# Attention scores from two fp32r parts of q and k instead of three bf16 parts, with the two kinds of scores in opposite halves of TensorE's rows

## The reference, cut to what matters

```python
qkv = jnp.einsum('bysd,ed->byse', x, w_qkv) + b_qkv          # (8, 1, 512, 768), fp32
q, k, v = jnp.split(qkv.reshape(B, S, 16, 48).transpose(0, 2, 1, 3), 3, axis=-1)
logits = jnp.einsum('bhqd,bhkd->bhqk', q, k) / math.sqrt(16)
vals = jnp.einsum('bhqk,bhkd->bhqd', jax.nn.softmax(logits, axis=-1), v)
out = jnp.einsum('bse,oe->bso', vals, w_out) + b_out
```

## Time and profile before

| | |
|---|---|
| median of three runs | 1222.1 us |
| the profiled execution | 1222.89 us, its span 1221.0 us |
| stage 1, projections | 0 to about 108 us |
| attention, 32 units | 108 to about 502 us; units 0 to 29 from 108.06 to 474.06 us |
| recurrence and shared expert | about 502 to 836 us |
| routed experts | 836 to 1221 us |
| PE busy, whole span | 1157.2 us (95%) |
| DVE, ACT, POOL busy | 800.3, 505.6, 395.0 us |
| granted TensorE clock, mean | 0.985 |

### The profile page before, as it was taken

How to read it: one execution, slowest core, us unless ns; L and a number is a source line. 1 busy time by engine, 2 the same in 40 slices (tenths; PEclk the granted TensorE clock), 3 DMA queues, 4 the chain that set the end, 5 groups by cost and what they waited for, 6 DMA issues and landing times.

```text
span 1221.0 us, 20443 instructions
## 1 busy us (share of the span) xinstructions
PE 1157.2 (95%) x5606; PEld 696.1 (57%) x5607; DVE 800.3 (66%) x1404; ACT 505.6 (41%) x890; POOL 395.0 (32%) x515
## 2 busy tenths in 40 slices
PE   6998999999999999889999999887999999999996
PEld 3654333333333334456655666556888888888885
DVE  3688888888888887677787778875333333333332
ACT  3445777777777777422112121431221122222221
POOL 3002621111111111224224433263444455544443
PEclk9998999999999999989999999998999999999998
DMA  8884333332333331124125542212333333333332
GB/s 297 257 274 163 84 89 84 89 100 72 99 89 82 90 83 56 70 87 104 32 73 104 104 87 46 59 36 44 52 52 52 52 52 48 51 48 51 52 52 35
DMA packets 108685, 105.32 MB, mean 86 GB/s; under 512 B 42464, under 2 KB 97904, under 8 KB 108624
## 3 DMA queue, kind: packets, MB, share of 16 engines
q1 hardware_dynamic: 90528, 81.18, 23.8%
q0 software_dynamic: 18112, 23.57, 11.4%
HBM read 64.88 MB, written 39.68 MB: 86 GB/s over the span
## 4 chain that ended last, share of the span: by engine, by line
PE 68%; DVE 9%; issue 6%; POOL 3%; DMA 3%; ACT 1%; another core or an unknown queue 1%; SPq 0%; POOLq 0%; DVEq 0%; ACTq 0%
PE mix_pairs L73 16%; PE mix_made L1707 10%; PE pv L673 10%; PE by_key L662 10%; PE by_query L653 8%; PE mix_made L1196 3%; PE mix_pairs L1234 3%; PE mix_turn L1700 3%; PE mix_turn L1680 1%; POOL kept_table L1081 1%; PE by_query L694 1%; PE mix_pairs L1226 1%; DMA out_rows<-mix_h 1%; PE mix_made L1213 1%; DVE k_mix_u L1388 1%
## 5 line engine op out<-in xcount | busy, mean ns | idle before, releaser
L746 DVE TENSOR_REDUCE k_neg_max<-by_query 128x2 f32<-128x1024 f32 x240 | 282.8, 1219 | 55.7 <-PE by_query L653 54.9
L806 ACT ACTIVATE k_wu_e<-by_key 128x512 f32<-128x512 f32 x512 | 278.5, 600 | 84.8 <-PE by_key L662 81.3
L662 PE MATMUL by_key<-k_wg_e 99*128 99x512 bf16 x512 | 180.5, 386 | 3.1 <-DVE pv L782 3.0
L1659 POOL DMA_INDIRECT out_rows<-x_y,k_slot x72 | 114.0, 1583 | 177.7 <-DVE x_y L1787 159.8
L1748 ACT ACTIVATE x_gate<-mix_pairs 128x512 f32<-128x512 f32 x72 | 43.0, 597 | 307.8 <-PE mix_pairs L73 307.8
L653 PE MATMUL by_query<-k_wg_e 96*128 96x512 bf16 x480 | 145.0, 383 | 0.3
L1707 PE MATMUL mix_made<-k_wd_e,x_acts_T 128*128 x576 | 136.0, 379 | 0.8 <-ACT x_acts_T L1757 0.8
L673 PE MATMUL pv<-k_wu_e,k_wd_e 128*17 128x512 f32 x1024 | 134.5, 598 | 0.2 <-ACT k_wu_e L806 0.2
L73 PE MATMUL mix_pairs<-w_short,x_T 128*128 x288 | 133.9, 465 | 0.0
L662 PEld LDWEIGHTS by_key<-k_wg_e 99*128 99x128 bf16 x512 | 42.4, 97 | 144.3 <-ACT k_wu_e L806 81.0
L1707 PEld LDWEIGHTS mix_made<-k_wd_e,x_acts_T 128*128 128x128 f32 x576 | 108.8, 189 | 18.8 <-issue 1.0
(11 more groups left out here) (220 smaller groups left out, 1779.1 us busy)
## 6 DMA issues: line engine op xcount, KB each, us to landing
k_wg_e<-kept_qk SPq DMA_DIRECT2D x384, 64.0 KB, 2.1
kept_qk<-k_qk_parts SPq DMA_DIRECT2D x32, 384.0 KB, 3.4
kept_v<-k_v_ones SPq DMA_DIRECT2D x8, 544.0 KB, 5.5
k_wd_e<-kept_v SPq DMA_DIRECT2D x32, 136.0 KB, 2.7
k_wu_e<-in_xT POOLq DMA_DIRECT2D x8, 512.0 KB, 6.9
kept_heads<-k_wd_e SPq DMA_DIRECT2D x8, 512.0 KB, 3.0
k_heads_in<-kept_heads SPq DMA_DIRECT2D x8, 512.0 KB, 10.8
k_wg_e<-in_wg_e SPq DMA_DIRECT2D x8, 512.0 KB, 4.9
```

The source lines that it names most:

```text
L662: pe.matmul(by_key[:, key_bank(job), :], k_rows[0:SROWS, g, h, kt * P:(kt + 1) * P], q_rows[0:SROWS, g, h, :], start=True, stop=True).then ...
L746: dve.tensor_reduce(neg_max[:, g % 2, 2 * n:2 * n + 2], by_query[:, bank:bank + 2, :], AX.X, ALU.max, negate=True).then_inc(query_read, 1)
L806: act.activation(probs[:, key_tile(j) // 2 * G + j // 2 % G, j % 2, :], by_key[:, key_bank(job), :], ACT.Exp, scale=float(HD) ** -0.5).the ...
L1659: pool.indirect_dma_start(out=dram["out"], in_=y[:, r % 2, :], in_offset=None, compute_op=ALU.add, out_offset=bass.IndirectOffsetOnAxis(ap ...
```

## The change

q and k are cut into two fp32r parts instead of three bf16 parts, and three products are added instead of six: a unit's rows are 48 for scores by query and 50 for scores by key, in fp32. Rows of units g = 0 and 1 start at partition 0, those of units 2 and 3 at partition 64. Since by_key works on unit g and by_query on unit g + 2, the two kinds of scores always stand in different halves of the rows. The third row of the maximum, the middle part (ACT) and the low part (DVE) go, and two of POOL's four steps in `split_max`. The order on PE becomes by_key, two by_query, by_key, by_key, two by_query, by_key; `MAX_BEHIND` is 6, `turn_heads` stands ahead of the queries of j = 12, and `copy_pv` follows j = 8. A unit's rows come in six transfers of 128 KB. In stage 1 a tile's parts take 512 KB to store instead of 384 KB, and PE waits for the same subtraction as before. DVE's pair maxima in stage 1 move behind other steps (`TAKE_BEHIND`). `q_rows` and `k_rows` get memory of their own in the place that the short weights use later; `max_parts` and `max_rows` lie in `wd_e`. Ones are set by two memsets of 32 partitions x 4096 fp32 instead of one of 3 partitions x 8192 bf16, and SyncE waits for them after the stores of batch 0.

```diff
-PARTS = 3
-Q_PART = (0, 0, 0, 1, 1, 2)
-K_PART = (0, 1, 2, 0, 1, 0)
+PARTS = 2
+Q_PART = (0, 0, 1)
+K_PART = (0, 1, 0)
+HALF = P // 2
-MAX_BEHIND = 3
+MAX_BEHIND = 6
...
+def rows_of(g, count=HALF, first=0):
+    return slice(HALF * (g // 2) + first, HALF * (g // 2) + count)
...
-    sp.dma_start(rows[HD * n:HD * (n + 1), g, :, :],
+    sp.dma_start(rows[rows_of(g, HD * (n + 1), HD * n), g % 2, :, :],
...
 def split_max(pool, mem, rows, done, base, step):
     pool.sem_inc(step)
-    pool.tensor_copy(mem["max_parts"][:, 0, :], rows).then_inc(done, 1)
+    pool.tensor_copy(short(mem["max_parts"][:, 0, :]), rows).then_inc(done, 1)
     pool.wait_ge(done, base + 1)
-    pool.tensor_tensor(mem["neg_rest"][:, :], rows, mem["max_parts"][:, 0, :], ALU.subtract).then_inc(done, 1)
...
-        TAKE_BEHIND = {b: (("rest", 0), ("low", 0), ("low", 2)) for b in (B - 5, B - 4, B - 1)}
+        TAKE_BEHIND = {b: (("rest", 0), ("rest", 2), ("v", 1)) for b in (B - 5, B - 4, B - 1)}
...
-            pool.memset(mem["k_rows"][KROWS:SROWS, :, :, :], 1.0).then_inc(ones_set, 1)
+            for half in range(2):
+                pool.memset(mem["k_rows"][HALF * half + HALF // 2:HALF * (half + 1), :, :, :], 1.0).then_inc(ones_set, 1)
...
             store(0)
+            sp.wait_ge(ones_set, 4)
...
-                    pe.wait_ge(qk_out[j], b)
+                    pe.wait_ge(cut[j], b)
...
-            def middle_part(b, j):
-                act.wait_ge(qk_out[j], b + 1)
-                act.activation(qk_parts[:, j, 1, :], qk_rest[:, j, :], ACT.Copy).then_inc(middle_made, 1)
...
-                dve.scalar_tensor_tensor(qk_rest[:, j, :], qk_ps[:, j, :], bqk[:, j:j + 1], qk_parts[:, j, 0, :],
-                                         ALU.add, ALU.subtract).then_inc(qk_out[j], 1)
-
-            def low_part(b, j):
-                dve.wait_ge(middle_made, 4 * b + j + 1)
-                dve.tensor_tensor(qk_parts[:, j, 2, :], qk_rest[:, j, :], qk_parts[:, j, 1, :],
-                                  ALU.subtract).then_inc(cut[j], 1)
+                dve.scalar_tensor_tensor(short(qk_parts[:, j, 1, :]), qk_ps[:, j, :], bqk[:, j:j + 1], qk_parts[:, j, 0, :],
+                                         ALU.add, ALU.subtract).then_inc(cut[j], 1)
...
-    QUERIES = (0, 2, 2, 0)
+    QUERIES = (2, 0, 2, 0)
     TURN_HEADS = 12
+    COPY_PV = 8
...
-                      q_rows[0:KROWS, g, h, t * P:(t + 1) * P], k_rows[0:KROWS, g, h, :],
+                      short(q_rows[rows_of(g, KROWS), g % 2, h, t * P:(t + 1) * P]), short(k_rows[rows_of(g, KROWS), g % 2, h, :]),
                       start=True, stop=True).then_inc(query_scored, 1)
...
-            pe.matmul(by_key[:, key_bank(job), :], k_rows[0:SROWS, g, h, kt * P:(kt + 1) * P],
-                      q_rows[0:SROWS, g, h, :], start=True, stop=True).then_inc(key_filled, 1)
+            pe.matmul(by_key[:, key_bank(job), :], short(k_rows[rows_of(g, SROWS), g % 2, h, kt * P:(kt + 1) * P]),
+                      short(q_rows[rows_of(g, SROWS), g % 2, h, :]), start=True, stop=True).then_inc(key_filled, 1)
...
-            ("qk", (B, 2, PARTS, D, S), BF16), ("v", (B, P, TT * H * VW), FP32), ("heads", (B, P, TT * D), FP32),
+            ("qk", (B, 2, PARTS, D, S), FP32), ("v", (B, P, TT * H * VW), FP32), ("heads", (B, P, TT * D), FP32),
```

More of the change, by code:

```diff
@@ L166, in stage_qkv @@
         x_used = [sem(f"x_used{n}") for n in range(2)]
-        qk_out = [sem(f"qk_out{n}") for n in range(4)]
         cut = [sem(f"cut{n}") for n in range(4)]
@@ L256, in store @@
                         sp.wait_ge(parts_stored[j], 16)
-                        for n in range(ROW_LOADS // 4 * j, ROW_LOADS // 4 * (j + 1)):
+                        for n in LOAD_BEHIND[j]:
                             load_rows(sp, mem, dram, 0, unit, n)
@@ L285, in score_pair @@
                     h, t = k // TT, k % TT
[L286 to L287 removed]
+                    mm = pe.matmul(fold_ps[:, k % 2, :], short(q_rows[rows_of(g, KROWS), g, h, t * P:(t + 1) * P]),
+                                   short(k_rows[rows_of(g, KROWS), g, h, :]), start=True, stop=True)
                 mm.then_inc(pair_scored, 1)
@@ L354, in high_part, with high_parts @@
                 act.wait_ge(qk_made, 4 * b + j + 1)
-                act.activation(qk_parts[:, j, 0, :], qk_ps[:, j, :], ACT.Identity,
+                act.activation(short(qk_parts[:, j, 0, :]), qk_ps[:, j, :], ACT.Identity,
                                bias=bqk[:, j:j + 1]).then_inc(high_made, 1)
-            def middle_part(b, j):
-                act.wait_ge(qk_out[j], b + 1)
-                act.activation(qk_parts[:, j, 1, :], qk_rest[:, j, :], ACT.Copy).then_inc(middle_made, 1)
-            def high_and_middle(b):
-                high_part(b, 0)
-                for j in range(1, 4):
+            def high_parts(b):
+                for j in range(4):
                     high_part(b, j)
@@ L417, in cut_and_add @@
                 b = 2 * i + par
-                rest(b, 0)
-                take_pairs_behind(b, "rest", 0)
-                for j in range(1, 4):
+                for j in range(4):
                     rest(b, j)
                     take_pairs_behind(b, "rest", j)
-                    low_part(b, j - 1)
-                    take_pairs_behind(b, "low", j - 1)
-                low_part(b, 3)
                 dve.wait_ge(v_stored, 16 * b)
@@ L523, in turned_max @@
     def turned_max(bank):
-        return by_key[:, bank, 0:P // 2].bitcast(BF16)
+        return by_key[:, bank, 0:P]
     PAIRS = G * TT // 2
@@ L710, in unit @@
                 score_by_key(b, g, j)
+                if j == TURN_HEADS and prev:
+                    turn_heads(bp, gp)
                 for _ in range(QUERIES[j % 4]):
@@ L825, in unit @@
                     copy_max(b1, g1)
-                if j == 7 and not (isinstance(b, int) and b == 0 and g == 0):
+                if j == COPY_PV and not (isinstance(b, int) and b == 0 and g == 0):
                     if isinstance(b, int) and (b, g) == (0, 1):
@@ L1906, in program @@
             mem["w_short"] = later.enter_context(nc.sbuf_tensor("w_short", [P, E, 2, DC, F], FP32))
+        with ExitStack() as early:
+            for name in ("q_rows", "k_rows"):
+                mem[name] = early.enter_context(nc.sbuf_tensor(name, [P, NG // 2, G, S], FP32))
         until_cut = ctx.enter_context(ExitStack())
```

66 lines of the change are left out of this document (26 added, 40 removed).

## The result

The changed kernel takes 1227.78 us (median of 20 runs, 1224.77 to 1231.87) where the kernel before took 1224.61 us on the same chip (20 runs, 1220.27 to 1227.91): ratio 1.0029, 95% interval 1.0018 to 1.0040. The profiled execution has a span of 1225.9 us against 1221.0. The forecast was 1177.

What follows compares the result with a forecast made beforehand. PE bounds the kernel now, DVE next at 9.9 us a unit. From the profiled 1222.9 us, -49 (30 units), +0.8 (units 30 and 31) and +3.4 (stage 1) give 1178.1, less 0.8 for the median: 1177 us, forecast 1168 to 1186, range 1161 to 1213.

Steps and rivals of the forecast that it cites:

- Pace of one fp32r score, 0.23 us: Scores on PE: fp32r matmuls of 512 columns start 0.23 us apart, about 0.015 more than bf16.
- Pace of a pair side by side, 0.23 us: Attention on PE: two scores in different row halves together take 0.23 us, against 0.46 in a row.
- wrong if above 0.3: Sign for attention: the forecast is wrong if the pair pace is above 0.3 us.
- rivals 1 and 2: Attention: 1, scores run in a row, 1236 us, chance 0.16; 2, weight loads set the pace, 1211 us, chance 0.11.
- DVE's floor of 9.9 us a unit: Attention: eight DVE reductions and the normalising step take 9.9 us; no unit with pairs can be shorter.
- How much of DVE's bound is reached: Attention, step tracing when DVE frees pairs: a unit takes 10.5 us instead of 12.18, -49 us for 30 units.
- Wrong if ACT and not DVE ends PE's waits: Sign for attention: PE's idle time should be ended by DVE's reductions; if by ACT, the forecast is wrong.
- Units 30 and 31, +0.8: Last two units, without pairs: slower score pace and changes of form, +0.5 to +1, taken as +0.8 us.
- Stage 1, +3.4: Stage 1: pace +0.5, going in and out of a half +1.6, DMA +2, tail -0.7 make +3.4 us.
- The DMA term (+2): Stage 1: larger stores add 14% of bytes where DMA is near its limit; bounds 0 and 12, taken +2 us.
- rival 3: Stage 1: DMA holds it, costing the 12 us in full instead of 2; 1187 us, chance 0.08.
- Rival 5: Attention and stage 1: each change of form empties the array, 12 us and 5.1 instead of 1.6; 1193 us, chance 0.09.

Runs made afterwards that it cites:

- same_half: Changed kernel with by_key's and by_query's units in the same row half, so their scores run in a row; 1304.71 us, ratio 1.0702.
- short_max: Changed kernel with DVE's maxima taken over 256 of the 512 keys; 1224.59 us, ratio 1.0036.
- short_exp: Changed kernel with exponentials over only 256 of 512 queries from batch 1 on; 1214.69 us, ratio 0.9963.
- full_end: wide_loads with by_key of units 30 and 31 also over all 128 rows, the idle half of q zeroed by POOL; 1215.25 us, ratio 0.9959.
- wide_loads: Changed kernel with stage 1's early pairs over all 128 rows and unit 3's rows loaded in attention's own program; 1218.67 us, ratio 0.9987.
- order_only: Kernel before, with its old bf16 scores, given only the changed kernel's order of PE's and ACT's work; 1216.71 us, ratio 0.9971.
- half_some: full_end with each pv split into two lots of 256 query columns, except the unit's first own pv; 1210.76 us, ratio 0.9955.
- wide_pairs: Changed kernel with stage 1's early pairs over all 128 rows and unit 3's rows loaded at stage 1's end; 1223.66 us, ratio 1.0038.
- half_pv: Changed kernel with every pv split into two lots of 256 query columns behind separate by_key products; 1241.71 us, ratio 1.0161.

## Why the prediction was wrong, step by step

- *Pace of one fp32r score, 0.23 us:* right (same_half: 0.23). *Pace of a pair side by side, 0.23 us:* right, 0.24, and "wrong if above 0.3" did not happen; rivals 1 and 2 fall. The Trainium skill (TensorE: Matmul & The Clock Gate, Part 3) states that tiles in distinct row groups run concurrently; the trace agrees, with by_key and by_query both starting at 330.61 us.
- *DVE's floor of 9.9 us a unit:* the sum is right by its rows, and short_exp shows DVE's maxima close behind. But short_max shows that it set nothing here. ***How much of DVE's bound is reached* is the step that failed.** It followed one ring, the pairs of by_query banks that DVE frees, and left out the other, the three by_key banks that ACT frees, because ACT's total (9.0 us) lay below DVE's. A total bounds throughput; the ring bounds latency: 0.54 to the start of the exponential, 0.60 of it and 0.05 to the load for every three gaps. It could have been read beforehand: in the rows of before an exponential starts 0.42 us behind its by_key (318.92 to 319.34) and lasts 0.60, 1.02 us in all, while the forecast's three gaps, at 0.23 us a pair, come to 0.7. "Wrong if ACT and not DVE ends PE's waits" is what happened. By quarters, in the unit from 330.61 to 342.46 us: plain 2.59 us where I had 2.39; with turned maxima 3.08 (333.20 to 336.28) where I had 2.65, since the turn takes a place in the same ring (it waits for ACT at 334.44); the half with the heads 2.66 + 3.52 = 6.18 where I had 5.5. Sum 11.85 against 10.54 (the mean unit is 11.88).
- The heads' quarter carries a second miss, smaller: PE waits 0.6 us in each unit, 17.3 us over 29, for DVE's normalising. I had let it cost DVE's time only, with PE far enough ahead, though the earlier trace rows show the wait in the kernel before (0.53 us at 326.29).
- *Units 30 and 31, +0.8:* measured +5.6. Mis-sized: I priced the pace and left "changes of form" at a token. *Stage 1, +3.4:* measured +7.7. Mis-sized above all in changes of form: 1.6 forecast and at most 3.5, measured 6.2 by the batches (full_end and wide_loads, without them, start attention at 110.40 and 109.41 us against 115.77). My bound came from the two gaps around pv, 0.09 and 0.13 us, and pv is a full-row product between full-row products of before (bf16, 96 to 99 of the 128 rows, and fp32, 128): no row of before held a change between half and full rows, and I took the nearest ones as its upper end, which they are not. The pace (+0.5) and the tail (-0.7) are right. The DMA term (+2) is nothing by the batches, and rival 3 falls; in its place stand 1.2 us of waiting for the moved pair maxima, for which the forecast has no term. That these small terms were forecast at 1.8 and came to some 1.4 is luck.
- Rival 5 (each change of form costs) had the kind right and the size for stage 1 (5.1) nearly so. The Trainium skill (TensorEngine Tiling (Array Packing), Key Properties) states that a change of tiling mode drains TensorE; the trace agrees, with 0.3 us more for a way in and out in attention, and 0.39 in stage 1. The rival still gave 1193 us, as it lacked the ring.
- *What the order alone is worth* I had folded into waits that go away (about 0.4 us a unit in rival 1). order_only shows 0.11 in the steady unit.

Together: of -49 us forecast for the 30 units, 8.7 came; the rest, 40 us or 1.34 a unit, lies 0.20 in the plain quarter, 0.43 in the one with the turned maxima and 0.68 in the half with the heads. The second ring, changes of form inside the unit and the wait for the heads share it. How much is each one's isn't settled; short_exp, which shortens the ring from 1.19 to 0.96, gives back 0.37 a unit before DVE's maxima hold PE.

## What to carry to other kernels

For every buffer ring between two engines write down the latency from the producer's start to the consumer's end and divide it by the number of buffers: an engine that is idle a quarter of its time can still set the pace, and a large block (pv) that falls into one gap of the ring does not hide the wait in the others. A change of row form on PE has a price at both ends; where half-row products stand alone between full-row ones, padding them with zero rows is cheaper (0.39 us a pair in stage 1; full_end gained back what the change lost, and 0.4% more). When a change bundles a new order with a new mechanism, run the order alone: here it was faster than the whole change.

## What the hardware showed that I had not expected

Two half-row fp32r products cost what one does (0.24 us), but the first pair behind a full-row product costs 0.34, and the step from a half-row to a full-row product 0.42. At the join of stage 1 and attention PE idles 2.3 us (2.97 before), and near the end of this idle time (at 114.7 us in short_exp, whose attention starts at 114.66; at 113.4 in full_end, 3 us behind its start at 110.40) its clock is granted at half, 1.2 GHz, and stays there though PE is busy again: for 10 us in the changed kernel (0.53 as the mean of 116.6 to 127.6), 7 before, 20 in half_some, 31 in wide_pairs, 37 in half_pv and 85 in same_half, where PE was busy in every microsecond of it. In all of them PE had stood idle at the join; what ends the stretch no run here isolates. Moving one unit's loads past the join (wide_pairs against wide_loads) changed the kernel by 5 us: in the profiles attention starts 5.3 us earlier and the stretch at half clock is 17 us instead of 31.
